# First layer: all key-norm blocks as Gram blocks on VectorE; second layer: softmax denominators by all-ones products

## What is computed

```
k = (ctx @ Wk).reshape(B, Skv, 16, 128)
k = k * rsqrt(mean(k * k, axis=-1) + eps) * gk        # layer 2 only
attn = softmax(q @ k^T * scale);  out = attn @ v;  x = x + out @ Wo
```

## Time and profile before

| | us |
|---|---|
| median of three runs | 2382.12 (2378.26 to 2382.53) |
| profiled execution | 2376.87 |
| its span, first to last instruction | 2375.1 |
| PE busy | 2218.0 (93%) |
| DVE busy | 1570.5 (66%) |
| POOL busy | 1405.8 (59%) |
| ACT busy | 827.6 (35%) |
| granted TensorE clock, mean | 0.972 |

### The profile page before, as it was taken

One profiled execution on the slowest core, in us unless ns is written; L12 is line 12 of the kernel. 1 busy time (PEld: TensorE's weight loads), 2 busy tenths in 40 slices (PEclk: granted clock), 3 DMA queues, 4 the chain that ended last, 5 costly groups with the idle time before them and its releaser, 6 DMA issues. The chain is left out here.

```text
span 2375.1 us, 27437 instructions
## 1 busy us (share of the span) xinstructions
PE 2218.0 (93%) x9314; PEld 1610.4 (68%) x9314; DVE 1570.5 (66%) x2570; ACT 827.6 (35%) x1751; POOL 1405.8 (59%) x1145
## 2 busy tenths in 40 slices
PE   8899999999999999999997598799999999976998
PEld 5477777777777777777774343477777777744887
DVE  2588888888888888888871689444444444404666
ACT  2233333333333333333331144334434344311332
POOL 0288887888777888877880000577777777602221
PEclk9799999999999999999998899899999999997999
DMA  2100000000000000000003000111011111010111
GB/s 86 52 21 20 27 27 14 26 13 27 27 27 14 27 14 27 27 27 14 1 1 150 0 0 0 66 52 53 27 52 46 33 52 33 7 69 14 40 46 36
DMA packets 14706, 76.79 MB, mean 32 GB/s; under 512 B 1698, under 2 KB 2178, under 8 KB 13218
## 3 DMA queue, kind: packets, MB, share of 16 engines
q1 hardware_dynamic: 14578, 75.18, 9.4%
HBM read 74.26 MB, written 0.92 MB: 32 GB/s over the span
## 5 line engine op out<-in xcount | busy, mean ns | idle before, releaser
L469 POOL TENSOR_TENSOR l_prod<-l_prod 125x256 f32<-125x256 f32 x672 | 483.9, 739 | 227.9 <-DVE l_prod L531 225.3
L531 DVE TENSOR_TENSOR l_prod<-l_side,l_xq 125x512 f32<-125x512 f32 x672 | 460.5, 685 | 92.7 <-PE l_side L661 87.0
L412 ACT ACTIVATE l_probs<-l_slots,mask_bias 125x448 f32<-125x448 f32 x384 | 240.8, 635 | 567.9 <-PE l_slots L603 567.7
L815 DVE TENSOR_TENSOR l_scaled<-l_slots,rk 125x896 f32<-125x896 f32 x192 | 209.6, 1091 | 308.8 <-PE l_slots L868 306.6
L795 POOL TENSOR_TENSOR l_acc<-l_acc,l_probs 125x896 f32<-125x896 f32 x160 | 337.5, 2109 | 116.6 <-ACT l_probs L757 114.1
L660 PE MATMUL l_side<-norm_lo,l_chi 128*125 128x512 f32 x768 | 379.5, 494 | 5.4 <-DVE l_prod L531 5.3
L612 PE MATMUL l_psO<-l_probs,l_nat 125*128 125x448 f32 x768 | 349.0, 538 | 0.0
L463 POOL TENSOR_TENSOR l_acc<-l_acc,l_probs 125x896 f32<-125x896 f32 x160 | 338.1, 2113 | 0.0
L879 PE MATMUL l_psO<-l_probs,l_nat 125*128 125x448 f32 x768 | 320.1, 539 | 2.1 <-ACT l_probs L757 2.1
L757 ACT ACTIVATE l_probs<-l_scaled 125x896 f32<-125x896 f32 x192 | 182.7, 952 | 348.5 <-DVE l_scaled L815 336.7
L661 PE MATMUL l_side<-norm_hi,l_chi 128*125 128x512 f32 x768 | 302.5, 394 | 0.0
(11 more groups left out here) (181 smaller groups left out, 3725.8 us busy)
## 6 DMA issues: line engine op xcount, KB each, us to landing
l_land<-in_ctxT SPq DMA_DIRECT2D x32, 750.0 KB, 4.3
l_nat<-in_ctxN SPq DMA_DIRECT2D x32, 750.0 KB
post_we<-in_experts SPq DMA_DIRECT2D x20, 384.0 KB, 3.1
pre_wqT<-in_wqT SPq DMA_DIRECT2D x1, 2048.0 KB, 7.3
mid_wo<-in_wo SPq DMA_DIRECT2D x1, 2048.0 KB, 10.7
mid_fac<-in_factors SPq DMA_DIRECT2D x1, 2048.0 KB, 15.3
mid_wq<-in_wq SPq DMA_DIRECT2D x1, 2048.0 KB, 20.2
post_wo<-in_wo SPq DMA_DIRECT2D x1, 2048.0 KB, 9.5
```

What stands on the lines that cost most here:

```text
L412: act.activation(P[t % NP][:, HALF * i:HALF * i + HALF], bank_of("S", t, i)[0:KT, 0:HALF], ACT.Exp, bias=m.mask_bias[:, b, t:t + 1]).then_ ...
L469: pool.tensor_tensor(buf[:, :, 0:C // 2], buf[:, :, 0:C // 2], buf[:, :, C // 2:C], ALU.add).then_inc(s.half_sum, 1)
L531: dve.tensor_tensor(prod[g % NPROD][:, :, :], bank, xt.unsqueeze(1).to_broadcast([KT, 4, C]), ALU.mult).then_inc(s.side_dve, 1)
L815: dve.tensor_tensor(scaled[t % 2][:, :].rearrange("p (a h q) -> p a h q", a=2, q=QS), src, rk.to_broadcast([KT, 2, H // 2, QS]), ALU.mult) ...
```

## The change

In the first layer the six A jobs a batch become N jobs, so there are 48 N; the weights for A and their loading go, ACT has no side jobs, and STEPS is written anew. In the second layer the sums are made by two products of 448 columns with a matrix of ones, which leave every denominator on all 128 partitions; DVE inverts them there, two times 128x448, into SBUF, and multiplies the output by them in two halves; `spread` goes. Dropped semaphores and a smaller norm_hi and norm_lo are left out here.

```diff
-DVE_G = 3
-BLOCKS = [(t, g) for t in range(NT) for g in range(DVE_G + t % 2)]
-SQUARED = [t for t in range(NT) if t % 2 == 0]
-NBLK, NSQ = len(BLOCKS), len(SQUARED)
+BLOCKS = [(t, g) for t in range(NT) for g in range(NG)]
+NBLK = len(BLOCKS)
...
-STEPS = ["MNMANM", "MNMNNM"] + ["NMNAMNM", "NMNNMNM"] * 2 + ["NNMANMN", "NNMNNMN", "NNMANMN", "NTNNTNN", "NANNNN", ""]
+STEPS = ["MNMNM", "MNMNNMN", "NMNNMNNM", "NMNNMNM", "NMNNMNNM", "NMNNMNM", "NNMNNMN", "NNMNNMN", "NNMNNMN", "NTNNTNN", "NNNN", ""]
...
-            STEP_JOBS[b, t] = [add(kind, b + 1 if kind in "MT" else b) for kind in STEPS[t] if kind in "NA" or b + 1 < B]
-    assert all(made[kind, b] == n for b in range(B) for kind, n in zip("MTNA", (2 * NT, 2, NBLK, NSQ)))
+            STEP_JOBS[b, t] = [add(kind, b + 1 if kind in "MT" else b) for kind in STEPS[t] if kind == "N" or b + 1 < B]
+    assert all(made[kind, b] == n for b in range(B) for kind, n in zip("MTN", (2 * NT, 2, NBLK)))
...
-        wk1 = sb("wk1", [C, 512], F32)
...
-            sp.dma_start(wk1[:, :], a.wk1).then_inc(s.ld_w1, 16)
...
-            act.wait_ge(s.ld_w1, 32)
-            act.activation(m.norm_hi[:, NG * 512:], wk1[:, :], ACT.Copy).then_inc(s.w_hi, 1)
...
-            dve.wait_ge(s.w_hi, 1)
-            dve.tensor_tensor(m.norm_lo[:, NG * 512:], wk1[:, :], m.norm_hi[:, NG * 512:].bitcast(F32),
-                              ALU.subtract).then_inc(s.const, 1)
...
-            if JOBS[n].kind == "A":
-                eng.wait_ge(s.side_act, number(n, "A"))
-            else:
-                eng.wait_ge(s.side_dve, number(n, "MTN"))
+            eng.wait_ge(s.side_dve, number(n, "MTN"))
...
-            def norms(n):
-
-                b, t = JOBS[n].b, SQUARED[JOBS[n].i]
-                act.wait_ge(s.side_pe, n + 1)
-                if t == 0:
-                    need(act, s.rk_pre, b)
-                bank = side[n % 3]
-                for c in range(4):
-                    sq = bank[0:KT, 128 * c:128 * c + 128]
-                    last = act.activation(sq, sq, ACT.Square, accum_out=msq[:, t, 12 + c:13 + c])
-                last.then_inc(s.side_act, 1)
...
-                    for n in STEP_JOBS[b, t]:
-                        if JOBS[n].kind == "A":
-                            norms(n)
...
-                    t, g = BLOCKS[i] if kind == "N" else (SQUARED[i], NG)
+                    t, g = BLOCKS[i]
                     keys, cols = slice(KT * t, KT * t + KT), slice(512 * g, 512 * g + 512)
-                    if kind == "A":
-                        pe.matmul(bank[0:KT, :], clo[b % 2][:, keys], m.norm_hi[:, cols], start=True, stop=False)
-                    pe.matmul(bank[0:KT, :], chi[b % 2][:, keys], m.norm_lo[:, cols], start=kind == "N", stop=False)
+                    pe.matmul(bank[0:KT, :], chi[b % 2][:, keys], m.norm_lo[:, cols], start=True, stop=False)
...
@@ second_attention
+        inv = sb("inv", [C, 2, HALF], F32)
...
             def invert(b):
 
                 dve.wait_ge(s.den, b + 1)
-                dve.reciprocal(m.inv[0:QBLK, :], norm_banks[0:QBLK, 0, 0:TT]).then_inc(s.inv, 1)
+                need(dve, s.o_done, 2 * b)
+                for half in range(2):
+                    dve.reciprocal(inv[:, half, :], norm_banks[:, half, 0:HALF]).then_inc(s.inv, 1)
 
             def normalise(b):
 
                 dve.wait_ge(s.o_raw, b + 1)
                 o = m.qs[:, bass.ds(b, 1), :, :].rearrange("p o (a h) q -> p (o a) (h q)", a=2)
-                dve.wait_ge(s.spread, 2 * b + 2)
-                dve.tensor_tensor(o, norm_banks[:, :, 0:HALF], o, ALU.mult).then_inc(s.o_done, 1)
+                for half in range(2):
+                    dve.wait_ge(s.inv, 2 * b + half + 1)
+                    dve.tensor_tensor(o[:, half, :], inv[:, half, :], o[:, half, :], ALU.mult).then_inc(s.o_done, 1)
...
             def sums(b):
 
                 pe.wait_ge(s.acc, (NT - 1) * (b + 1))
-                need(pe, s.o_done, b)
-                for j in range(QBLK):
-                    last = pe.matmul(norm_banks[:, 0, 0:TT], m.row_of[0:KT, 127 - j:255 - j], acc[:, TT * j:TT * j + TT],
-                                     start=j == 0, stop=j == QBLK - 1)
+                need(pe, s.inv, 2 * b)
+                for half in range(2):
+                    last = pe.matmul(norm_banks[:, half, 0:HALF], m.ones[0:KT, :], acc[:, HALF * half:HALF * half + HALF],
+                                     start=True, stop=True)
                 last.then_inc(s.den, 1)
-
-            def spread(b):
-
-                pe.wait_ge(s.inv, b + 1)
-                for half in range(2):
-                    for j in range(4):
-                        last = pe.matmul(norm_banks[:, half, TT * j:TT * j + TT], m.ident[:, 4 * half + j:4 * half + j + 1].to_broadcast([128, 128]), m.inv[:, :],
-                                         start=True, stop=True)
-                    last.then_inc(s.spread, 1)
 
             def body(b, par, nxt, nxt2):
                 start = isinstance(b, int) and b == 0
                 for t in range(NT):
-                    if t == 1 and not start:
-                        spread(b - 1)
...
-            spread(B - 1)
```

More of the change, by code:

```diff
@@ L58, in plan @@
         for t in range(NT):
-            STEP_JOBS[b, t] = [add(kind, b + 1 if kind in "MT" else b) for kind in STEPS[t] if kind in "NA" or b + 1 < B]
-    assert all(made[kind, b] == n for b in range(B) for kind, n in zip("MTNA", (2 * NT, 2, NBLK, NSQ)))
+            STEP_JOBS[b, t] = [add(kind, b + 1 if kind in "MT" else b) for kind in STEPS[t] if kind == "N" or b + 1 < B]
+    assert all(made[kind, b] == n for b in range(B) for kind, n in zip("MTN", (2 * NT, 2, NBLK)))
 plan()
-COUNTS = {kinds: list(itertools.accumulate(job.kind in kinds for job in JOBS)) for kinds in ("A", "N", "MTN")}
+COUNTS = {kinds: list(itertools.accumulate(job.kind in kinds for job in JOBS)) for kinds in ("N", "MTN")}
 def number(n, kinds):
@@ L145, in before_attention @@
     s = semaphores(sem, tag, LN_SEMAPHORES + ["ld_x", "ld_mask", "ld_const", "ld_w0", "ld_w1", "const", "ready", "on_act", "on_dve", "xnT",
-                 "fold", "w_hi", "g_hi", "mcount"])
+                 "fold", "g_hi", "mcount"])
     jobs = [("act", "fold", i) for i in range(8)]
@@ L248, in _ @@
                     if i == 0:
-                        pe.wait_ge(s.ld_w1, 32)
+                        pe.wait_ge(s.ld_w1, 16)
                     for c in range(4):
@@ L293, in first_attention @@
         "scores", "probs", "pv", "acc", "den", "inv", "spread", "o_raw", "o_done",
-        "side_pe", "side_dve", "side_act", "half_sum", "ksum", "rk_pre"])
+        "side_pe", "side_dve", "half_sum", "ksum", "rk_pre"])
     NP = 3
@@ L373, in high_parts @@
                     act.wait_ge(s.scores, 2 * NT * (b - 1))
-                    act.wait_ge(s.side_pe, last_of(b - 2, "NA") + 1)
+                    act.wait_ge(s.side_pe, last_of(b - 2, "N") + 1)
                 act.activation(chi[b % 2][:, :], land[:, :], ACT.Copy).then_inc(s.ctx_hi, 1)
@@ L383, in nat_high @@
                 act.activation(xq[:, :, :], nat[b % 2][:, :, :], ACT.Copy).then_inc(s.nat_hi, 1)
-            def norms(n):
-                b, t = JOBS[n].b, SQUARED[JOBS[n].i]
-                act.wait_ge(s.side_pe, n + 1)
-                if t == 0:
-                    need(act, s.rk_pre, b)
-                bank = side[n % 3]
-                for c in range(4):
-                    sq = bank[0:KT, 128 * c:128 * c + 128]
-                    last = act.activation(sq, sq, ACT.Square, accum_out=msq[:, t, 12 + c:13 + c])
-                last.then_inc(s.side_act, 1)
             def norms_out(b):
                 act.wait_ge(s.ksum, NBLK * (b + 1))
-                act.wait_ge(s.side_act, NSQ * (b + 1))
                 act.activation(m.rk[:, b, :, :], msq[:, :, :], ACT.Copy, bias=RMS_EPS, scale=1.0 / HD).then_inc(s.rk_pre, 1)
@@ L696, in second_attention @@
         "ld_land", "ld_nat0", "ld_nat1", "ctx_hi", "ctx_lo", "q_hi", "q_lo", "scores", "scaled", "probs", "pv", "acc",
-        "den", "inv", "spread", "o_raw", "o_done"])
+        "den", "inv", "o_raw", "o_done"])
     LAG, NP = 2, 3
@@ L1398, in build @@
             m.valid = for_first("valid", [128, B], F32)
-            m.norm_hi = for_first("norm_hi", [C, (NG + 1) * 512], F32R)
-            m.norm_lo = for_first("norm_lo", [C, (NG + 1) * 512], F32R)
+            m.norm_hi = for_first("norm_hi", [C, NG * 512], F32R)
+            m.norm_lo = for_first("norm_lo", [C, NG * 512], F32R)
             with_norm_buffers(before_attention, "pre", nc, m, a, "pre", sem)
@@ L1437 @@
         "wq1": chunks(i["L1_xattn_Wq"]), "wkT1": heads(i["L1_xattn_Wk"], 16), "wvT1": heads(i["L1_xattn_Wv"], 16),
-        "wk1": c(i["L1_xattn_Wk"][:, 1536:]),
         "wo1": c(i["L1_xattn_Wo"].reshape(16, 128, 256).transpose(1, 0, 2)),
```

## The result

The changed kernel takes 2408.95 us (2407.94 to 2409.25, four runs) against 2382.32 for the kernel before: ratio 1.0117, 95% interval 1.0102 to 1.0132. It is slower by 26.6 us, where +7 was forecast. That is inside the stated range (2364 to 2415), but above the band of 2382 to 2400 to which the forecast itself gave its chance of one half. The profiled execution took 2407.94 (span 2406.2).

A forecast was written before the change was run, and what follows sets the result against it. PE was taken to bound the kernel, with little room on DVE and POOL. First layer +32, second layer -27, its end +2.6 and first stage -0.5 summed to +7: 2390 us in medians, range 2364 to 2415.

The forecast's parts named there:

- R3: First layer, steps 5 to 9: DVE as the bound, +15 to +28 on the forecast, 2405, up to 2418; chance 0.14.
- Bound of before, slots: First attention: PE sets the time, busy 71.32 of 71.70 us; slots are the spacing of instructions in a full queue.
- Removal of the A products, -2.2 a batch: First layer: PE loses 1.40 us of products and 0.8 of A's bank coming free late, together -2.2 a batch.
- Stalls of steps 0, 2, 3 and 4, +4.5: First layer: PE waits for banks because POOL's lumps delay DVE, +4.5 us a batch.
- the chain read in step 4 of before: First layer: last multiply of step 3, through POOL's queue and DVE's reduction and maximum, to the freed bank: 7.4 us.
- From step 5 on ... I find no further wait: First layer, step 5 onward: POOL's lumps are an add of 2.07 us, and no further wait was found.
- Last batch, -2.2: First layer's last batch: it has no M, T or context slices and gains 2.2 us.
- Second layer, -27: Second attention: cheaper sums and no spread, less a 0.2 us stall behind reciprocals: -1.8 a batch, 15 times, -27.
- First stage, -0.5: First stage: dropped weight load, its copy on ACT and difference on DVE save 0.5 us, bounds -1 and 0.
- R1: Rival: PE alone counts and all work fits in sum, -60, 2322 us; chance 0.12.
- R2: Rival: only POOL's own total holds in steps 2 to 4, +1.1 a batch, 2371 us (2364 to 2383); chance 0.18.
- R4: Rival, second layer: normalise's second half held by POOL's add, PE waits about 1.5, 15 times, +22, 2412; chance 0.06.

The follow-up runs named there:

- The mended kernel: Changed kernel with reduction three N behind, two halvings ahead of POOL's low part, last add ahead of step 10's last two halvings, second-layer reciprocals apart: 2327.12 us, ratio 0.9772.
- Lag 3: Changed kernel with the product reduced three N jobs behind its multiply instead of two, and five product buffers: 2353.34 us.
- the order of POOL's queue: Changed kernel where POOL halves a step's first two products before its low part and the others after it: 2376.18 us.
- the last add early: Changed kernel where POOL makes a batch's last add before the last two halvings of step 10: 2396.58 us.
- the reciprocals apart: First layer as before, second as changed, but one wide reciprocal before and one behind tile 3's scaling, normalise behind tile 4's: 2353.07 us, ratio 0.9882.

## Why the prediction was right or wrong

- **The outcome**: the side (slower) and the mechanism (POOL's lumps hold DVE, DVE holds PE) were right; the size was not, +26.6 for +7. The time fell inside the range because the range was wide enough for the rivals, and it fell where R3 had put it (2405 to 2418), though R3's mechanism was not what happened: that part is luck. (The terms as added give 2389; the forecast says 2390.)
- **Bound of before, slots**: right. The starts worked out from them came within 0.3 us of the rows.
- **Removal of the A products, -2.2 a batch**: too large; it was about -1.6. The mended kernel has 70.78 for 72.05, 1.27 less, while its wait in step 0 is 0.70 for 0.38. Added back, that gives 1.6: the products' 1.40 and 0.2 for the banks that came late, not the 0.8 that was read from one step.
- **Stalls of steps 0, 2, 3 and 4, +4.5**: the mechanism and the places were right. In the batch shown PE's idle times there are 0.62, 1.17, 0.22 and 1.70, together 3.3 more than before's 0.38. With the 0.27 that each wait costs beyond its idle time (0.17 and 0.1, as for the last add above), I estimate +4.1. Lag 3 and the order of POOL's queue shorten the period at equal work; both point to the chain read in step 4 of before.
- **"From step 5 on ... I find no further wait"**: this is the step that failed. Through steps 5 to 9 it held. But at the end POOL had the four halvings of step 10 ahead of its last add, and the sums on PE waited for that add: an idle time of 0.51 on PE in every batch (557.35), where before had none except in the last batch. By the same estimate it cost 0.8. A second wait is smaller: the second N of step 10 starts at 548.72, 0.46 behind the product ahead instead of 0.20, as it had to wait for a late multiply to free its bank; with the restart some 0.3. I followed POOL only as far as DVE needed it, and not to its second customer.
- **The period, 74.4 for 75.5**: the terms as measured are 0.6 for the removal, -0.4 for the stalls, +0.8 and +0.3 for the two waits at the end. They add up to 1.3, for the 1.1 to be found, about 16 us in all. One batch took 77.16: behind its stall of 1.81 in step 4 the granted clock was 0.77 over 7.31 us (last section).
- **Reductions waiting for POOL, 3 to 4 us a batch**: 5.3 in the batch shown. Steps 2 to 4 have 3.5, the rest is in steps 7 to 11.
- **Last batch, -2.2**: -0.8 (64.03 for 64.83). Its sums waited 2.83 for the last add, as before (2.80), and then took 2.64 for 2.04. With the last add early they waited 1.47, and the batch took 62.08.
- **Second layer, -27**: -29.2. The period after was as forecast, 34.35 for 34.4; before's was 36.3 where the slots had given 36.1. The reciprocal from PSUM took 2.93, the end came out as worked out, and half of normalise took 0.61.
- **First stage, -0.5**: PE's products there ended 1.4 later instead, and executions of equal code differ by 1.6 there. No run here can show the 0.5.
- **Rivals**: R1 and R2 fell as forecasts for this kernel, though the mended one shows that what R1 wanted (all work fits in sum) was true and only the order forbade it. R3 fell: steps 6 to 8 took PE's slots, 5.9 each, and DVE at the same load fits in 70.8. R4 did not occur, by 0.08 us.

## What to carry to other kernels

When work moves to an engine that has room, write out its queue in order, with every consumer of every result in it: here both the room (DVE busy 61, POOL 58 of 72 us before) and the loss (4.7 us a batch, which another order gave back) were real. Look for a lump that stands ahead of short pieces others wait for, and ask how many pieces later the result is read; one more job of lag, and the buffer it needs, was worth 3 us a batch. Follow the queue to its end: the last add, read by PE and not by DVE, was the wait left out here. Two edits of opposite sign in one change hide each other: time each half alone.

## What the runs showed of the hardware

The hold between DVE and POOL moved to another instruction. Since tile 3's exponential comes late, POOL's adds stand back to back until the middle of the batch (1746.78 to 1760.77 in the batch above), and DVE's low part of the queries, which has two SBUF inputs, takes longer: a mean of 2.44 us where it was 1.66. With the reciprocals apart it is 1.66 again. The scores behind it kept their 2.7 us steps, so it cost nothing.

```profile
L791 DVE TENSOR_TENSOR l_qlo<-qs,l_qhi 128x896 fp32r<-128x896 f32 x16 | 39.0, 2437 | 9.2 <-ACT l_qhi L717 9.2
```

TensorE's clock fell twice in the changed kernel's first attention. The stretch from 667.69 follows waits of 0.62, 1.19, 0.19 and 1.81 us in the 32.7 us before it; the other batches had the same waits, the last of about 1.7, and kept 1.00. Its mean of 0.77 lies between the two levels, 2.4 GHz (1.00) and 1.2 GHz (0.50). The second row is behind the last batch, all at the lower level; PE had been idle 2.83 and 0.94 us around the sums. The third row is the same place in the kernel before, with idle times of 2.80 and 0.94, and there the clock stayed up.

```profile
667.69:675.00 7.31, 7.31 (x24) 5.67 (x25) 6.22 (x13) 1.27 (x2) 5.53 (x7) 0.77 0.00 1
1304.84:1310.16 5.32, 3.75 (x16) 3.49 (x16) 2.10 (x3) 0.00 (x0) 0.00 (x0) 0.50 0.00 0
1250.76:1254.35 3.59, 2.04 (x16) 1.86 (x16) 2.09 (x3) 0.00 (x0) 0.00 (x0) 1.00 0.00 0
```

In these rows a reciprocal costs by its columns and not by its partitions: 8x112 took 0.85 us before, and 128x448, with 4 times the columns and 16 times the partitions, takes 2.93. A multiply of 128x448 takes 0.61. The Trainium skill (VectorE: DVE Perf Modes, First, the fixed hardware budget) says that the reciprocal is an iterative divide in the pipe; it gives no time. The rows here do give it; how the engine divides they do not show.
